# Padding the 64 hidden units of the last expert layer to 128

## What is computed

```
def _L3_ffn_ref(x, router_w, router_b, W1, b1, W2, b2):     # W1 (32, 256, 64), W2 (32, 64, 256)
    logits = xf @ router_w.T + router_b
    idx = jnp.argmax(logits, axis=-1)
    h = jnp.einsum('nd,ndh->nh', xf, w1t) + jnp.take(b1, idx, axis=0)
    h = jax.nn.relu(h)
    out = jnp.einsum('nh,nhd->nd', h, w2t) + jnp.take(b2, idx, axis=0)
    out = jax.nn.relu(out)
```

## Time and profile before

| | us |
|---|---|
| median of 3 runs | 6865.72 |
| the profiled execution's own time | 6862.74 |
| its span, first to last instruction | 6861.0 |
| `dense` of the last layer | about 6548 to 6600 of the span |
| `routed_ffn` of the last layer | about 6640 to 6817 of the span |
| `combine` and the store of the result | from there to 6861 |

### The profile page before, as it was taken

The page is one execution under the profiler, slowest core; times in us unless marked ns, Lnnn a source line. Parts: engine busy times, 40 slices in busy tenths (PEclk is TensorE's granted clock), DMA queues, the critical chain, the costliest instruction groups (busy, mean ns, idle before and its releaser), DMA issues. The chain is left out here.

```text
span 6861.0 us, 87557 instructions
## 1 busy us (share of the span) xinstructions
PE 5084.8 (74%) x21976; PEld 3349.2 (49%) x21977; DVE 2850.6 (42%) x6134; ACT 1150.4 (17%) x2799; POOL 2280.6 (33%) x2415
## 2 busy tenths in 40 slices
PE   5519169996939887677577777486979797979857
PEld 3415057446924576443355433254968343434433
DVE  4456189204250132556587466677141202020142
ACT  2312046001300122111101111001222101010020
POOL 2771610461527123277522377521014000000014
PEclk9999999996969978888889888898979898989955
DMA  0000023434634245499854599764036432414234
GB/s 15 2 1 1 20 93 144 142 129 130 211 132 154 74 140 185 137 306 307 246 179 142 173 306 307 211 208 126 0 122 194 143 136 80 149 54 161 68 81 120
DMA packets 477265, 949.51 MB, mean 138 GB/s; under 512 B 111984, under 2 KB 285403, under 8 KB 474653
## 3 DMA queue, kind: packets, MB, share of 16 engines
q1 hardware_dynamic: 325308, 638.92, 27.5%
q0 software_dynamic: 114208, 281.05, 13.6%
q10 hardware_dynamic: 37568, 27.34, 1.4%
HBM read 732.28 MB, written 214.82 MB: 138 GB/s over the span
## 5 line engine op out<-in xcount | busy, mean ns | idle before, releaser
L1150 PE MATMUL banks<-ring,xn 128*128 128x512 f32 (+1 forms) x3500 | 1358.9, 550 | 145.4 <-DMA ring<-adjacency 145.4
L1150 PEld LDWEIGHTS banks<-ring,xn 128*128 128x128 f32 x3500 | 629.1, 192 | 863.3 <-issue 715.9
L992 POOL DMA_INDIRECT rows<-pairs,idxr x832 | 806.7, 970 | 239.2 <-issue 216.5
L1877 PE MATMUL banks<-agg,hotT 128*128 x1664 | 634.7, 487 | 231.2 <-issue 222.3
L1731 POOL IOTA found_i<- 128x25 int32 x4 | 0.6, 148 | 1809.0 <-ACTq L1727 1389.0
L377 POOL DMA_INDIRECT bin_table<-bins_pay,bins_row x392 | 456.5, 1164 | 428.9 <-DVE nodes_row L767 153.4
L377 POOL DMA_INDIRECT dst_table<-nodes_pay,nodes_row x392 | 378.8, 966 | 643.1 <-DVEq L1118 474.3
L1877 PEld LDWEIGHTS banks<-agg,hotT 128*128 128x128 f32 x1664 | 306.3, 225 | 509.2 <-issue 500.6
L2130 PE MATMUL banks<-msg,hot 128*128 128x264 f32 x1664 | 426.0, 402 | 54.5 <-DVE msg L2100 37.3
L1850 DVE TENSOR_TENSOR prod<-banks,rows 128x512 f32<-128x512 f32 x416 | 267.7, 685 | 420.5 <-DMA rows<-pairs,idxr 279.4
L1603 PE MATMUL banks<-xT,w1r 128*128 128x128 f32 (+1 forms) x3088 | 417.2, 289 | 0.3 <-DMA w1r<-in_L_ffn_W 0.3
(11 more groups left out here) (350 smaller groups left out, 6804.1 us busy)
## 6 DMA issues: line engine op xcount, KB each, us to landing
ring<-adjacency SPq DMA_DIRECT2D x150, 1280.0 KB
spill<-rows SPq DMA_DIRECT2D x208, 512.0 KB
rows<-spill SPq DMA_DIRECT2D x208, 512.0 KB
w1r<-in_L_ffn_W SPq DMA_DIRECT2D x114, 512.0 KB
adjacency<-strips SPq DMA_DIRECT2D x13, 3200.0 KB
w1r<-in_L_ffn_w SPq DMA_DIRECT2D x65, 512.0 KB
rows<-home_rows SPq DMA_DIRECT2D x35, 640.0 KB
ring<-adjacency SPq DMA_DIRECT2D x25, 640.0 KB
```

The costliest lines, as they stand in the source:

```text
L992: nc.gpsimd.indirect_dma_start(rows[:, row, :], None, table, bass.IndirectOffsetOnAxis(ap=idxr[:, at + g:at + g + 1], axis=0))\
L1150: last = nc.tensor.matmul(K.ps[2 * (g % 2) + o][:, 0:wd], x[:, t * D + o * P:t * D + (o + 1) * P], ring[:, n % R, 0:wd // cols, q * SPAN_S ...
L1877: last = nc.tensor.matmul(K.ps[2 + 2 * (jj % 2) + g // 2][:, g % 2 * D:(g % 2 + 1) * D], hotT[:, jj % 2, g * P:(g + 1) * P], tile_of(q, t) ...
```

## The change

For an expert layer with fewer than 128 hidden units, all buffers of hidden units become 128 wide, the part that no DMA fills is set to zero, and the products take all 128 columns and rows:

- `w1r` grows from 64 to 128 columns for each place and half. VectorE clears `b1T` and all of `w1r` at the start of `routed_ffn`, ahead of its first copy.
- A new semaphore `cleared` holds back SyncE's first fetch and ScalarE's first DMA (`b1T`, and `bias2` behind it) until that is done. For the other three layers VectorE only raises the semaphore.
- GpSimd clears partitions 64 to 127 of `second` in `dense`, where it had nothing to do.

```diff
+            @block.gpsimd
+            def _(pool):
+                if ahead:
+                    ahead.clear()
...
-        self.second = st.sb("second", [self.hm, self.experts * (self.hid // self.hm) * D])
+        self.nc, self.second = st.nc, st.sb("second", [P, self.experts * (self.hid // self.hm) * D])
...
+    def clear(self):
+        if self.hm < P:
+            self.nc.gpsimd.memset(self.second[self.hm:P, :], 0.0)
...
+    wide = nh * P
...
-        w1r = st.sb("w1r", [P, R, KD, hid])
+        w1r = st.sb("w1r", [P, R, KD, wide])
...
-        hT = st.sb("hT", [hm, 2, nh * P])
+        hT = st.sb("hT", [P, 2, nh * P])
...
             @block.sync
             def _(sp):
+                sp.wait_ge(cleared, 1)
+
...
-                        sp.dma_start(w1r[:, j, :, :], w1v[:, bass.ds(e, 1), :, :].rearrange("p e k h -> p (e k) h")).then_inc(fetched[j], 16)
+                        sp.dma_start(w1r[:, j, :, 0:hid], w1v[:, bass.ds(e, 1), :, :].rearrange("p e k h -> p (e k) h")).then_inc(fetched[j], 16)
...
-                                last = nc.tensor.matmul(K.ps[2 + jj % 2][0:hm, h * P:(h + 1) * P],
-                                                        w1r[:, jj, s, h * hm:(h + 1) * hm],
+                                last = nc.tensor.matmul(K.ps[2 + jj % 2][:, h * P:(h + 1) * P],
+                                                        w1r[:, jj, s, h * P:(h + 1) * P],
...
-                act.dma_start(b1T[:, :], b1.rearrange("e (c p) -> p (e c)", p=hm)).then_inc(biased, 16)
+                act.wait_ge(cleared, 1)
+                act.dma_start(b1T[0:hm, :], b1.rearrange("e (c p) -> p (e c)", p=hm)).then_inc(biased, 16)
...
-                                                    K.ps[2 + j % 2][0:hm, h * P:(h + 1) * P], func,
+                                                    K.ps[2 + j % 2][:, h * P:(h + 1) * P], func,
...
             @block.vector
             def _(dve):
+                if hm < P:
+                    nc.vector.memset(b1T[:, :], 0.0)
+                    nc.vector.memset(w1r[:, :, :, :], 0.0).then_inc(cleared, 1)
+                else:
+                    dve.sem_inc(cleared, 1)
```

More of the change, by code:

```diff
@@ L1522, in __init__ @@
         self.hm = min(P, self.hid)
-        self.second = st.sb("second", [self.hm, self.experts * (self.hid // self.hm) * D])
+        self.nc, self.second = st.nc, st.sb("second", [P, self.experts * (self.hid // self.hm) * D])
         self.w2 = w2
         self.whole = st.sem("whole")
+    def clear(self):
+        if self.hm < P:
+            self.nc.gpsimd.memset(self.second[self.hm:P, :], 0.0)
     def fetch(self, act):
-        act.dma_start(self.second[:, :].rearrange("p (n d) -> p n d", d=D),
+        act.dma_start(self.second[0:self.hm, :].rearrange("p (n d) -> p n d", d=D),
                       self.w2.rearrange("e (c p) d -> p (e c) d", p=self.hm)).then_inc(self.whole, 16)
@@ L1541, in routed_ffn @@
     with stage(nc) as st:
-        b1T = st.sb("b1T", [hm, experts * nh])
-        w1r = st.sb("w1r", [P, R, KD, hid])
+        b1T = st.sb("b1T", [P, experts * nh])
+        w1r = st.sb("w1r", [P, R, KD, wide])
         bias2 = st.sb("bias2", [P, experts * D])
@@ L1551, in routed_ffn @@
         stored = [st.sem(f"stored{j}") for j in range(R)]
-        spread = st.sem("spread")
+        spread, cleared = st.sem("spread"), st.sem("cleared")
         biased, turned, copied, hidden, acted, summed, written = (
```

## The result

The changed kernel takes 6848.64 us (median of 9 executions, 6847.48 to 6857.41), the kernel before, measured beside it, 6865.34 (9 executions, 6863.51 to 6871.31). The ratio is 0.9977, with a 95% interval of 0.9968 to 0.9987: 16.7 us less. The forecast was 6849.1, and its border to "no change" was a gain of 0.2%; the measured gain is 0.23%, but the interval reaches down to 0.13%. The profiled execution took 6849.47 us, its span, first to last instruction, 6847.7.

A forecast was written before the change was run, and what follows sets the result against it. TensorE was taken to bound the last expert stage at 2.81 us a chunk. Terms -17.3 + 0.5 + 0.2 = -16.6 us took the profiled 6862.74 to 6846.1; 2.98 for the median gave 6849.1 us, range 6842 to 6858.

The forecast's parts named there:

- The bound before: Last expert stage: TensorE sets the pace at 2.81 us a chunk.
- The gaps at the shape borders: TensorE's step, last layer: 0.71 us lies at borders T to H, H to S2, S2 to T; 2.81 falls to 2.10.
- The first rival: Last stage: gaps come from TensorE's short queue, not shapes; pace stays 2.81 us, time 6867, no change; chance 7%.
- Weight loads: TensorE's loads for H and S2: wider loads add nothing, with 64 columns at 219 ns and 128 at 202 ns.
- The third rival: Last stage: H's wider loads double to 438 ns and bind, step 3.0 us, time 6877, slower; chance 3%.
- GpSimd is next, at 2.57: Last stage after the change: GpSimd's gather, scatter and 0.30 us before each set the pace, 2.57 us a chunk.
- The second rival: Last stage: TensorE sets the pace at the high clock, step about 1.1 us, time 6781; chance 3%.
- First to last scatter: Last expert stage, from first to last scatter: 135.2 us against 152.5, so -17.3 us.
- The start: Start of the last stage: memsets delay first fetches 1.0 us, 0.5 us of gaps vanish; first scatter +0.5 us.
- GpSimd's memset of `second`: In `dense`: at most 12.4 us, hidden while GpSimd does nothing, price 0; rival that it holds VectorE up 3%.
- The other expert layers: Other three expert layers: a semaphore VectorE raises at once, 0.1 us each at most, +0.2 us in all.
- own case: Whole program: forecast without rivals, bounds on start, end, pace and execution scatter giving 6844 to 6854; chance 84%.

The follow-up runs named there:

- e1: Kernel before, last expert stage scattering only every fourth chunk; TensorE's step 2.81 us, first to last scatter 146.3 us against 152.5; no total used.
- e5: Kernel before plus one one-column GpSimd memset ahead of each scatter of the last expert stage; 6865.52 us beside 6865.36.
- e3: Changed kernel with only H's columns padded, S2 at 64 rows, and every fourth chunk scattered; step 2.62 us at the low clock, no total used.
- e4: Changed kernel with only S2's rows padded, H at 64 columns, and every fourth chunk scattered; step 2.63 us at the low clock, no total used.
- e12: Changed kernel with only S2's rows padded, H at 64 columns, all scatters done; 6852.11 us against 6866.56 for the kernel before, ratio 0.9978.
- e2: Changed kernel, last expert stage scattering only every fourth chunk; pace 2.285 us a chunk, no total used.
- e11: Changed kernel plus four one-column GpSimd memsets ahead of each scatter; 7787.35 us on the pausing chip, gathers 2.62 to 2.65 us apart between pauses.
- e6: Changed kernel plus one one-column GpSimd memset ahead of each scatter; 6850.31 us, pace unchanged at 2.569 us.
- e8: Changed kernel clearing only `b1T` ahead of the DMAs and only the padding of `w1r`, SyncE not waiting; 6850.34 us, ratio to the kernel before 0.998.
- e9: Changed kernel with only H's columns padded, S2 at 64 rows, all scatters done; ratio to the kernel before 0.9996, on the pausing chip.
- e10: Changed kernel with only S2's rows padded, H at 64 columns, all scatters done; ratio to the kernel before 0.9991, on the pausing chip.

## Why the prediction was right, point by point

- **The bound before.** Right. e1 took three quarters of the scatters away and TensorE's step stayed at 2.81 us. That TensorE's line bound the stage is shown, and e5 shows the same from GpSimd's side.
- **The gaps at the shape borders.** Right: 2.14 us a step at the low clock, forecast 2.10. e3 and e4 show that the shapes make them, not the short groups or semaphores, which are the same there. The first rival (gaps stay) is out. What stays open is how the 0.71 us divides over the three borders: in e4 S2 still takes 1.02, though S2 and the T behind it have one shape. And closed gaps are enough for the gain but weren't needed for it: the changed kernel's clock rose to 0.89 as well, and e12, which keeps most of the gaps, has the same pace by its clock. No run has the gaps closed and the clock at 0.50 throughout; for that case there is only the step of 2.14 us, which is under 2.57. So that the closed gaps by themselves would have brought the whole gain is worked out, not measured.
- **Weight loads.** Right that they cost nothing, wrong in the reason. The prediction set T's loads (128 columns, 202 ns) beside H's (64 columns, 219 ns) and saw no growth. H's own loads do grow. At clock 0.50 throughout they take 334 ns on average in e3, where they have 128 columns, against 219:

```profile
L1616 PEld LDWEIGHTS banks<-xT,w1r 128*128 128x128 f32 x108 | 26.4, 334 | 0.0
...
L1615 PEld LDWEIGHTS banks<-xT,w1r 128*128 128x128 f32 x204 | 32.5, 227 | 6.3 <-issue 4.8 <-DMA w1r<-in_L_ffn_W 0.4
```

  The 227 ns of the changed kernel (second row) are mostly from the high clock: there the median load takes 192 ns with 128 columns and 137 with 64 (e12). The rule of the Trainium skill ("TensorE: Matmul & The Clock Gate", section on LDWEIGHTS) that the time of a load grows with its columns is borne out for H by these rows; T's 202 ns for the same 128 columns and clock show that the columns aren't all of it. The third rival fails at its other link: with loads of 334 ns, longer than the 0.21 us of a matmul record, H still takes 0.85 us and not the rival's 1.75, since they overlap each other as well (four cover 0.98 us in e3).
- **GpSimd is next, at 2.57.** Right (2.569). Once scatters are gone the pace falls (e2), and once GpSimd's line is longer than its spare room it grows (e11); both together show the bound. The reason that I gave for the 0.30 us was too simple (e6, e11). The second rival (TensorE sets the pace at the high clock) needed GpSimd to issue faster: the clock did rise, a step took 1.14 us where 1.1 was forecast, and nothing came of it.
- **First to last scatter.** Mis-sized: -16.0 us for -17.3. The steady part fits; the term that was off is the end. From the last gather to the last scatter I took 8.0 us and it is 9.37 (6791.18 to 6800.55), within the bounds 7.0 to 9.5. TensorE's T for that last chunk starts 3.86 us after the gather's issue:

```profile
6795.04 0.44 PE L1604 MATMUL banks<-ident,rows 128*128 128x128 f32 x2 [0.71 <-DMA rows<-table,idx]
```

  The 8.0 leaves 3.5 us for that, so 0.4 of the 1.4 us lie in the gather, which lands later than the 2.5 us of a scatter. The other 1.0 lies behind T: from there to the last scatter it is 5.51 us, and the sum has 1.1 + 3.4. It kept the prices of the low clock, less the gaps; why the stretch is longer although the clock was 1.00 there wasn't tested.
- **The start.** +0.9 for +0.5, inside its bounds. The two memsets cost 1.3 us at the first fetch (1.87 to 3.15 after the sorting), not 1.0:

```profile
6641.98 0.91 DVE L1659 MEMSET w1r<- 128x1024 f32 x1 [0.16 <-issue]
6643.61 1.43 ACTq L1640 DMA_DIRECT2D bias<-in_L_ffn_b  x1
```

  The second chunk's H comes 1.0 us later in the stage (20.43 after the sorting, before 19.41), which is the microsecond of the forecast. The term that was off is the 0.5 us of gaps said to vanish from that H to the first scatter: this takes 3.16 us before (6658.06 to 6661.22) and 3.07 after, and likewise 3.15 in e5, 3.04 in e6, 3.07 in e8. Only one H and one S2 lie on that way, with the one border between them, so 0.1 vanishes and not 0.5. The position itself scatters between executions by as much.
- **GpSimd's memset of `second`.** Right, it is free. It takes 6.92 us (bound 12.4) in `dense`, and TensorE's wait for the router's bias there is 5.74 us, before 5.67:

```profile
6549.72 6.92 POOL L1534 MEMSET second<- 64x8192 f32 x1 [1239.93 <-POOLq L130]
...
6568.46 1.06 PE L1375 MATMUL banks<-w,xT 128*128 128x32 f32 x4 [5.74 <-DMA b<-in_L_ffn_router_b]
```

- **The other expert layers.** +0.2 is below what can be read. VectorE's instructions, matched one to one between the two profiled executions, drift apart on the way (the changed kernel is 3.4 us early at 4000 us), and at 6147 us, behind all three layers, it is 0.4 us late.

The sum was -16.6 and the medians differ by 16.7. The two mis-sized terms (+1.3, +0.4) are small beside how far single executions lie apart (6847.48 to 6857.41), so this closeness is partly luck. The bounds that the prediction names for its own case also don't add up to its "6844 to 6854": summed they give 6844.3 to 6857.1, and the -0.3 for the end belongs to 7.7 us and not to the 7.0 of its lower bound. The range of 6842 to 6858 holds both.

## What to carry to other kernels

Where TensorE alternates between small products of different shapes, read the time from start to start at each border against the same code with one shape: padding with zeros can be worth more than the columns it wastes. At the low clock it brought 0.67 us a step with all three shapes alike, against 0.18 and 0.19 for the halves. Work out the next engine's line first, idle time between its instructions included; here it let through 0.24 of the 0.67 us a step that TensorE gained, and so half of the padding, with the clock that rose, did as well as all of it. To lower the time further, work would have to leave GpSimd's line: another short instruction there costs nothing until its 0.30 us are full.

## What was not expected of the hardware

- **The clock.** In the kernel before TensorE was busy throughout the stage and its granted clock stayed at 0.50 (1.2 GHz), and so in e1 and e5, and in e3 and e9 with H's columns filled. With S2's rows filled the clock rose within the stage, although the engine did less: 0.89 at 87 of 125 us busy in the changed kernel, 0.82 at 99 of 125 in e12, 0.88 at 54 of 70 in e4. All five traces without filled rows show 0.50 there and all nine with them 0.76 to 0.94. The added rows hold zeros. Why they count isn't known. I had left this open. In the changed kernel it gained nothing beyond the closed gaps, as GpSimd set the pace; in e12 it is what brings TensorE under GpSimd's 2.57.
- **A low reading of the clock without a cost.** In the profiled execution after, the granted clock reads 0.57 through the first 690 us, before it reads 1.00; the busy times of the stretch are alike (TensorE 384.69 us in the kernel before), and at 830 us VectorE is 1.6 us ahead of the kernel before, not behind it. Even in a stretch where TensorE is busy all the time its round takes the same: 4.10 us from L682 to L682 at 1.00 (600.86 to 604.96 before), 4.06 at 0.50 (599.77 to 603.83 after). Whether the low clock cost nothing there or the reading doesn't tell the engine's rate in this stretch, the traces don't say:

```profile
0.00:690.00 690.00, 383.54 (x3218) 253.19 (x3219) 370.64 (x634) 171.15 (x357) 329.43 (x267) 0.57 0.02 5
```

- **Pauses.** On the chip of e9 to e11 TensorE, ScalarE and VectorE stood still together for 2 to 3 us now and then, while GpSimd went on issuing: in e9 TensorE is idle for 2.21 us ahead of 7643.13, and a gather goes out at 7641.71. That stretched the mean pace of two different kernels (e9, e10) to the same 3.11 us and hid an effect that another chip showed clearly (e12). What pauses them isn't known.
